# SyncE's order of loads around the second score stack, and both token parts written in slots 14 and 15

## The chip, the cores and the metric

The kernel runs on one core of one Trainium2 chip. The metric is the device time of one execution in microseconds. Three runs of the kernel before give a median of 1288.39 us (1287.05 to 1291.39).

## The reference, cut to what matters

For each of 32 batches, x is 256 tokens by 512 channels and adj is 256 by 256:

```python
h = relu(layernorm(x, eps=1e-5))
q, k, v = (split_heads(h @ W.T) for W in (Wq, Wk, Wv))      # 16 heads of 32
a = (q @ k^T) * 512**-0.5 + (adj + adj)
a = where(row of a has any nonzero, a, -inf)
p = softmax(a);  p = where(isnan(p), 0, p)
out = x + (p @ v, heads joined) @ Wo.T
```

## The kernel before, in words

Every product is made to near float32 accuracy out of halves: a matrix is kept as a high part in 16 bits and a low part (what the high part lacks), and a product is three 16-bit products. The high part is made by ScalarE, the low part by VectorE. q and k are split into two float32r parts and stacked (96 rows of three head-sized blocks), so that one matmul per half of the tokens gives a head's scores.

A batch b is worked through in 16 slots, one for each head hh. In slot hh TensorE does, in this order: the transposes of head hh's probabilities (L490), the scores of head hh+3 (L476, which in slots 13 to 15 belong to batch b+1), in even slots the value products of the two heads before (L511, L512), and then pieces of the projections named in the table `JOBS` (L401): in slots 0 to 3 the last of batch b's q, k and v; in 4 to 7, 10, 11, 14 and 15 those of batch b+1; in 8, 9, 12 and 13 the output projection of batch b-1. So heads 0 to 7 need the first stack, heads 8 to 15 the second one, whose heads 8, 9, 10 and 11 are first wanted in slots 5, 6, 7 and 8.

VectorE does in slot hh: `shift` of head hh+2 (L995: scores into `minus` with the row's bound), every fourth slot `any_nonzero` (L1016), its part of the projections that ended (`take`: L914 and L916 for q and k, L922 for v), `low_probs` of head hh (L1004) and then the extras. The extras that matter here: `tokens_stats` and `moments_of` for batch b+2 in slot 7 (L834, L843), `low_tokens(b+2, 0)` in slot 14 and its other half `low_tokens(b+1, 1)` in slot 0 of the next batch (L974, writes h_parts from h and h_parts), `low_outputs(b, 0)` in slot 15 and `low_outputs(b-1, 1)` in slot 4 (L968, writes o_parts from o and o_parts).

ScalarE does the exponentials (L725), the high parts (L736 for probabilities, L705 for outputs, L746 for tokens), the copies of products out of PSUM, and in slot 13 `copy_adj(b+1)` (L754), which waits for the shift of head 15. GpSimd does `fold` (L1223 and L1229: the sums that tell whether a row has a nonzero), `divide` (L1187 to L1203) in slots 1, 5, 9 and 13, the residual additions (L1215) and `normalise` of batch b+2 (L1163 to L1179) in slot 7.

All DMAs are issued by SyncE, one after the other, in an order written out by hand; a wait in front of one holds all behind it. A stack is twelve DMAs from SBUF to SBUF (L269), three for each group j of heads; group j of the second stack serves heads 8+j and 12+j. `stack(1, b)` waits for the last q and k product to be taken in slot 2, and has `turn_outputs(b-1, 1)` in its middle: a transposing DMA (L305) that waits for `low_outputs(b-1, 1)`. The token loads, the residual's x, the stores of y and the loads of adj stand between the stacks. The synchronisation is by semaphores. SyncE's loop runs over two batches a turn, the loops of VectorE, ScalarE and GpSimd over one; TensorE's is written out in full.

Of the kernel before, what the change touches and what calls it, by code (L numbers as in the profile page):

```python
# [14 lines left out]
HEADS = 16  # L15
# [64 lines left out]
def attention_block(nc, x, adj, wq, wk, wv, wo_t, out):  # L80
    B, N, D = x.shape
    NT = N // P
# [21 lines left out]
    with ExitStack() as ctx:  # L104
# [122 lines left out]
        def settled(engine, name):  # L227


            engine.sem_inc(went_on[name], 1)  # L230
# [18 lines left out]
        def count(kind, n, b):  # L249

            return b * PER_BATCH[kind] + (n + 1)

        def head_no(b, hh):
            return b * HEADS + hh

        @block.sync
        def _(sp):
# [31 lines left out]
            def turn_tokens(b, t, odd, first):  # L289

                sp.wait_ge(h_split, (b - 1) * NT + (t + 1))
                settled(sp, "sp")
                if not first:

                    sp.wait_ge(ended["qk"], count("qk", 0, b - 1))
                    settled(sp, "sp")
                sp.dma_start_transpose(hT[odd][:, t, :, :], h_parts[:, t, :, :].rearrange("p a d -> p (a d)")
                                       ).then_inc(h_turned[t], 16)
# [10 lines left out]
            def load_tokens(b):  # L309

                sp.wait_ge(h_ready, b)
                settled(sp, "sp")
                sp.dma_start(x_in[:, :, :], x_d[b]).then_inc(x_loaded, 16)

            def load_adj(b):

                sp.wait_ge(adj_copied, b)
                settled(sp, "sp")
                sp.dma_start(adj_in[:, :, :], adj_d[b]).then_inc(adj_loaded, 16)
# [18 lines left out]

            def body(b, odd, first, last):
                ends = last or isinstance(b, int) and b + 2 == B  # L340
                if not (first or ends):
                    load_tokens(b + 2)
                if not (first or last):
                    turn_tokens(b + 1, 1, 1 - odd, False)
                if not (first or last):
                    load_adj(b + 1)
                stack(1, b, first)
                if first:
                    load_adj(1)
                if not last:  # L350
                    stack(0, b + 1, False)
                if not ends:
                    turn_tokens(b + 2, 0, odd, False)
                if not first:
                    store(b - 1, 0)
                    store(b - 1, 1)

                    sp.dma_start(x_res[:, :, :], x_d[b]).then_inc(res_loaded, 16)
                if not last:
                    turn_outputs(b, 0)  # L360

            def store(b, t):

                sp.wait_ge(y_ready, b * NT + (t + 1))
                settled(sp, "sp")
                sp.dma_start(out_d[b, :, t, :], y[:, t, :]).then_inc(stored[t], 16)  # L366

            body(0, 0, True, False)
            with sp.Fori(1, B - 3, 2) as b:
                body(b, 1, False, False)  # L370
                body(b + 1, 0, False, False)
            body(B - 3, 1, False, False)
            body(B - 2, 0, False, False)
            body(B - 1, 1, False, True)
            for t in range(NT):

                sp.wait_ge(last_y, t + 1)
# [251 lines left out]
        def _(act):  # L629
# [32 lines left out]
            def high_out_weight(k):  # L662

                act.wait_ge(wo_leveled, k + 1)
                nc.scalar.activation(wo_hi[:, k, :], wo_in[k // 2][:, k % 2, :], ACT.Copy).then_inc(wo_high, 1)
# [82 lines left out]
            def copy_adj(b):  # L748

                act.wait_ge(adj_loaded, (b + 1) * 16)  # L750
                if not (isinstance(b, int) and b == 0):

                    act.wait_ge(shifted, head_no(b, 0))
                nc.scalar.activation(adj_now[:, :, :], adj_in[:, :, :], ACT.Copy).then_inc(adj_copied, 1)  # L754
# [22 lines left out]
            def body(b, first, nearly, last):  # L777
                for hh in range(HEADS):
                    if hh % 2:

                        if hh > 1:
                            copy_outputs(b, hh // 2 - 1, first and hh < 10)
                        elif not first:
                            copy_outputs(b - 1, PAIRS - 1, False)
                    if hh == 4:

                        take("v", 3, b, first)
                    if hh == 14 and not first:

                        take("y", 1, b - 1)  # L790
                    if hh + 1 < HEADS:
                        exponentials(b, hh + 1, first and hh + 1 < 2)
                    elif not last:
                        exponentials(b + 1, 0, False)
                    for kind, n, d in ended_before(hh, first, last):
                        if (kind, n) in (("v", 3), ("y", 1)):
                            continue
                        take(kind, n, b + d, first and (kind, d) in (("v", 0), ("qk", 0)))
                    if first and 10 <= hh < 10 + KT:

                        high_out_weight(hh - 10)
                    if hh == HEADS - 3 and not (first or last):
                        copy_adj(b + 1)
                    high_probs(b, hh, first and hh < 4)
                    if hh == HEADS - 3 and first:
                        copy_adj(b + 1)
                    if first and hh == 0:
                        split_tokens(1, True)
                    if not first and hh == 3:
                        high_outputs(b - 1, 1)  # L810
                    if not (nearly or last) and hh == 11:
                        split_tokens(b + 2, False)
                    if not last and hh == 14:
                        high_outputs(b, 0)
# [14 lines left out]
        def _(dve):  # L829
            def tokens_stats(b, tiles):  # L830

                dve.wait_ge(x_loaded, (b + 1) * 16)
                for t in tiles:
                    end = nc.vector.bn_stats(stats[:, t, :], x_in[:, t, :])  # L834
                end.then_inc(stats_done, 1)

            def moments_of(b, steps):


                dve.wait_ge(stats_done, steps)  # L840
                settled(dve, "dve")
                for t in range(NT):
                    end = nc.vector.bn_aggr(mean_var[:, t, :], stats[:, t, :])  # L843
                end.then_inc(moments, 1)
# [126 lines left out]
            def low_tokens(b, t):  # L971

                dve.wait_ge(h_high, b)
                nc.vector.scalar_tensor_tensor(h_parts[:, t, 1, :], h[:, t, :], 0.0, h_parts[:, t, 0, :],  # L974
                                               ALU.max, ALU.subtract).then_inc(h_split, 1)
# [86 lines left out]
            def body(b, first, nearly, last):  # L1062
                for hh in range(HEADS):
                    if hh + 2 < HEADS:
                        shift(b, hh + 2, first and hh + 2 < 4, first and hh + 2 < 8)
                    elif not last:
                        shift(b + 1, hh + 2 - HEADS, False)

                    if hh % 4 == 1 and not (first and hh == 1):
                        any_nonzero(*((b, hh // 4 - 1) if hh > 1 else (b - 1, QUADS - 1)), first and hh < 12)  # L1070
                    for kind, n, d in ended_before(hh, first, last):
                        take(kind, n, b + d)
                    low_probs(b, hh, first and hh < 2)
                    if not (nearly or last):
                        if hh == 7:
                            tokens_stats(b + 2, range(NT))
                            moments_of(b + 2, b + 3)
                        if hh == 14:
                            low_tokens(b + 2, 0)
                    if not first and hh == 4:  # L1080
                        low_outputs(b - 1, 1)
                    if not last and hh == 15:
                        low_outputs(b, 0)
                    if first and hh == 4:
                        out_weight_extent(1)
                        out_weight_top()
                    if first and hh == 6:
                        out_weight_scale()
                    if not (first or last) and hh == 0:
                        low_tokens(b + 1, 1)  # L1090
                    if first and hh in (1, 2):
                        low_tokens(1, hh - 1)

# [230 lines left out]
```

## Time and profile before

| what | value |
|---|---|
| median of three runs | 1288.39 us |
| the profiled execution's own time | 1287.51 us |
| its span | 1285.7 us |
| granted TensorE clock, mean | 0.993 |
| PE busy | 1191.1 us (93%) |
| DVE busy | 1082.4 us (84%) |
| ACT busy | 1026.1 us (80%) |
| POOL busy | 917.0 us (71%) |
| packets of the DMA queue that SyncE feeds | 65.2% of 16 engines' span |

Times in the rows are microseconds from the start of the span; PE is TensorE's matmul and PEld its weight load, DVE is VectorE, ACT ScalarE, POOL GpSimd, SP SyncE. 1.8 us of the profiled execution lie outside the span, and its time is 0.9 us below the median. A batch takes about 38.8 us, so 0.1 us a batch is about 3 us in all. Slot 0 of batch 15 begins at 621.18 in the trace, slot 0 of batch 16 at 659.14.

### The profile page before, as it was taken

The page shows a single profiled execution, that of the slowest core. Times are in us where ns is not written, and L with a number is a line of the kernel's source. Part 1 is how long each engine was busy: PE and PEld are TensorE (multiplying, and loading weights), DVE is VectorE, ACT ScalarE, POOL GpSimd, SP SyncE. Part 2 cuts the span into 40 slices and gives each one's busy share as a digit, 9 for nine tenths or more (in the row PEclk, how much of TensorE's full clock was granted, in tenths as well). Part 3 has the DMA queues.
Part 4 walks back from the last instruction along what each step waited for, and adds up shares of the span by engine and source line. Part 5 has one row for each costly group of instructions (what it writes and reads, how often), then busy time and mean ns, then how long its engine had stood idle before and what let it go on. Part 6 is the DMA issues. An engine that isn't in the chain of part 4 may idle for free. (4 is left out here: it accounts for less than half of the span.)

```text
span 1285.7 us, 41724 instructions
## 1 busy us (share of the span) xinstructions
PE 1191.1 (93%) x12609; PEld 998.5 (78%) x12609; DVE 1082.4 (84%) x3509; ACT 1026.1 (80%) x2399; POOL 917.0 (71%) x1272
## 2 busy tenths in 40 slices
PE   6889999999999999999999999999999999999997
PEld 5778777787778778778878777878777877777884
DVE  7888888888888888888888888888888888888885
ACT  5778887888788788877888878888877887878884
POOL 5586776777777677767777767777776777776765
PEclk9899999999999999999999999999999999999998
DMA  6566567676577675577766577765686765677742
GB/s 217 121 148 159 131 144 184 152 177 149 120 159 170 159 175 140 139 163 156 173 166 142 134 175 152 177 153 141 134 189 147 182 154 137 137 180 153 165 121 83
DMA packets 222901, 197.95 MB, mean 154 GB/s; under 512 B 146113, under 2 KB 155841, under 8 KB 222785
## 3 DMA queue, kind: packets, MB, share of 16 engines
q1 hardware_dynamic: 222784, 196.16, 65.2%
q8 instruction: 103, 1.69, 0.6%
q14 instruction: 14, 0.11, 0.0%
HBM read 46.14 MB, written 16.78 MB: 49 GB/s over the span
## 5 line engine op out<-in xcount | busy, mean ns | idle before, releaser
L725 ACT ACTIVATE probs<-minus,bounds 128x256 f32<-128x256 f32 x1024 | 464.1, 506 | 79.4 <-DVE bounds L995 78.7
L1223 POOL TENSOR_TENSOR fold<-minus 128x512 f32<-128x512 f32 x256 | 325.9, 1273 | 233.2 <-DVE bounds L995 233.0
L1004 DVE TENSOR_TENSOR pT_lo<-pT_ps,pT_hi 128x512 f16<-128x512 f32 x512 | 346.8, 677 | 120.5 <-ACT pT_hi L736 117.8
L995 DVE CUSTOM_DVE_ANT_0 minus<-s_ps,adj_now 128x256 f32<-128x256 f32 x1024 | 388.3, 415 | 9.1 <-issue 6.4
L736 ACT ACTIVATE pT_hi<-pT_ps 128x512 f16<-128x512 f32 x512 | 304.4, 595 | 65.4 <-PE pT_ps L490 62.8
L401 PE MATMUL job_ps<-hT,w_hi 128*128 128x256 f16 x2048 | 351.4, 273 | 2.9 <-DMA hT<-h_parts 2.5
L490 PE MATMUL pT_ps<-ident,probs 128*128 128x128 f32 x2048 | 309.1, 274 | 4.0 <-ACT probs L725 3.8
L476 PE MATMUL s_ps<-qk_stack 96*128 96x256 f32 x1024 | 249.5, 325 | 47.1 <-DMA qk_stack<-qk_parts 46.7
L401 PE MATMUL job_ps<-hT,w_lo 128*128 128x256 f16 x1024 | 279.4, 273 | 0.0
L490 PEld LDWEIGHTS pT_ps<-ident,probs 128*128 128x128 f32 x2048 | 244.7, 142 | 33.4 <-ACT probs L725 5.1
L1229 POOL TENSOR_TENSOR bounds<-fold 128x256 f32<-128x256 f32 x256 | 195.0, 762 | 25.1 <-POOL fold L1223 9.6
L476 PEld LDWEIGHTS s_ps<-qk_stack 96*128 96x128 f32 x1024 | 155.3, 192 | 63.0 <-DMA qk_stack<-qk_parts 62.6
L401 PEld LDWEIGHTS job_ps<-hT,w_hi 128*128 128x128 f16 x2048 | 181.0, 98 | 28.0 <-DVE v_parts L922 3.0
L401 PE MATMUL job_ps<-w_hi,hT 128*128 128x256 f16 x1016 | 193.6, 274 | 0.2 <-DVE qk_parts L916 0.2
L511 PE MATMUL o_ps<-v_parts,pT_hi 128*128 128x65 f16 x2048 | 164.1, 193 | 24.7 <-DVE pT_lo L1004 24.3
L401 PE MATMUL job_ps<-wo_hi,oT 128*128 128x512 f16 x512 | 174.6, 382 | 0.4 <-DVE oT L1102 0.3
L511 PEld LDWEIGHTS o_ps<-v_parts,pT_hi 128*128 128x128 f16 x2048 | 125.7, 97 | 44.4 <-DVE pT_lo L1004 32.2
L512 PE MATMUL o_ps<-v_parts,pT_lo 128*128 128x33 f16 x2048 | 156.4, 179 | 0.0
L401 PE MATMUL job_ps<-w_lo,hT 128*128 128x256 f16 x508 | 138.9, 274 | 0.0
L512 PEld LDWEIGHTS o_ps<-v_parts,pT_lo 128*128 128x128 f16 x2048 | 129.3, 96 | 0.1
L401 PEld LDWEIGHTS job_ps<-w_hi,hT 128*128 128x128 f16 x1016 | 97.0, 98 | 19.1 <-DVE qk_parts L916 6.3
L401 PEld LDWEIGHTS job_ps<-hT,w_lo 128*128 128x128 f16 x1024 | 100.1, 98 | 12.0
(102 smaller groups left out, 1615.5 us busy)
## 6 DMA issues: line engine op xcount, KB each, us to landing
qk_stack<-qk_parts SPq DMA_DIRECT2D x756, 128.0 KB, 2.4
x_in<-x SPq DMA_DIRECT2D x32, 512.0 KB, 4.5
x_res<-x SPq DMA_DIRECT2D x32, 512.0 KB, 4.1
out<-y SPq DMA_DIRECT2D x64, 256.0 KB, 2.3
adj_in<-adj SPq DMA_DIRECT2D x32, 256.0 KB, 4.1
qk_stack<-qk_parts SPq DMA_DIRECT2D x24, 64.0 KB, 2.0
w_in<-wq SPq DMA_DIRECT2D x2, 512.0 KB, 6.4
w_in<-wk SPq DMA_DIRECT2D x2, 512.0 KB, 8.0
```

The costliest lines, as they stand in the source:

```text
L401: end = nc.tensor.matmul(dst, lhs[a](k), rhs[c](k), start=i == 0, stop=i == len(terms) - 1)
L476: end = nc.tensor.matmul(s_ps[SCORE_BANK[hh]][:, t * N:(t + 1) * N], stack[:, 0, t * P:(t + 1) * P], stack[:, 1, :], start=True, stop=True)
L490: end = nc.tensor.transpose(pT_ps[hh % 2][:, m * N + t * P:m * N + (t + 1) * P], probs[hh % 2][:, t, m * P:(m + 1) * P], ident[:, :])
L511: nc.tensor.matmul(ps[:, 0:LOW + HD], hi, v[:, 0:LOW + HD], start=m == 0, stop=False)
L512: end = nc.tensor.matmul(ps[:, 0:HD + 1], lo, v[:, 0:HD + 1], start=False, stop=m == NT - 1)
L725: end = nc.scalar.activation(probs[hh % 2][:, t, :], minus[hh // 2 % 2][:, hh % 2, t, :], ACT.Exp, bias=bounds[:, hh // 2 % 4, 2 * (hh % 2 ...
L736: nc.scalar.activation(pT_hi[hh % 4][:, :, :], pT_ps[hh % 2][:, :].rearrange("p (m n) -> p m n", m=NT), ACT.Copy).then_inc(pT_high, 1)
L995: end = nc.vector.tensor_tensor_reduce(out=minus[pair % 2][:, hh % 2, t, :], in0=s_ps[SCORE_BANK[hh]][:, t * N:(t + 1) * N], in1=adj_now[: ...
L1004: nc.vector.tensor_tensor(pT_lo[hh % 4][:, :, :], pT_ps[hh % 2][:, :].rearrange("p (m n) -> p m n", m=NT), pT_hi[hh % 4][:, :, :], ALU.sub ...
L1223: nc.gpsimd.tensor_tensor(f1[:, :, :], src[:, :, 0:N // 2], src[:, :, N // 2:N], ALU.add).then_inc(folded1, 1)
L1229: nc.gpsimd.tensor_tensor(f2, f1[:, :, 0:N // 4], f1[:, :, N // 4:N // 2], ALU.add).then_inc(folded2, 1)
```

## The change

On SyncE, the three steps that stood ahead of the second stack go elsewhere. The token load and the load of adj run one batch further ahead (b+3 in place of b+2, b+2 in place of b+1) and come after the first stack; both transposing DMAs of batch b+2's tokens are issued together, between the two stores of y. On VectorE the second half of the token parts moves from slot 0 of the next batch to slot 15, where it comes before `low_outputs(b, 0)`; the first half stays in slot 14. One of the two tiles of the statistics moves from slot 7 to slot 3. On ScalarE `copy_adj` comes after `high_probs` in slot 13 in place of before it. Nothing of the arithmetic changes.

```diff
@@ SyncE
             def body(b, odd, first, last):
                 ends = last or isinstance(b, int) and b + 2 == B
-                if not (first or ends):
-                    load_tokens(b + 2)
-                if not (first or last):
-                    turn_tokens(b + 1, 1, 1 - odd, False)
-                if not (first or last):
-                    load_adj(b + 1)
                 stack(1, b, first)
                 if first:
                     load_adj(1)
                 if not last:
                     stack(0, b + 1, False)
-                if not ends:
-                    turn_tokens(b + 2, 0, odd, False)
+                if not (ends or isinstance(b, int) and b + 3 == B):
+                    load_tokens(b + 3)
                 if not first:
                     store(b - 1, 0)
+                if not ends:
+                    load_adj(b + 2)
+                    for t in range(NT):
+                        turn_tokens(b + 2, t, odd, False)
+                if not first:
                     store(b - 1, 1)
                     sp.dma_start(x_res[:, :, :], x_d[b]).then_inc(res_loaded, 16)
...
-            with sp.Fori(1, B - 3, 2) as b:
+            with sp.Fori(1, B - 5, 2) as b:
                 body(b, 1, False, False)
                 body(b + 1, 0, False, False)
-            body(B - 3, 1, False, False)
-            body(B - 2, 0, False, False)
-            body(B - 1, 1, False, True)
+            for b in range(B - 5, B):
+                body(b, b % 2, False, b == B - 1)
@@ ScalarE
-                    if hh == HEADS - 3 and not (first or last):
-                        copy_adj(b + 1)
                     high_probs(b, hh, first and hh < 4)
-                    if hh == HEADS - 3 and first:
+                    if hh == HEADS - 3 and not last:
                         copy_adj(b + 1)
@@ VectorE
                     low_probs(b, hh, first and hh < 2)
                     if not (nearly or last):
+                        if hh == 3:
+                            tokens_stats(b + 2, range(0, 1))
                         if hh == 7:
-                            tokens_stats(b + 2, range(NT))
-                            moments_of(b + 2, b + 3)
-                        if hh == 14:
-                            low_tokens(b + 2, 0)
+                            tokens_stats(b + 2, range(1, NT))
+                            moments_of(b + 2, 2 * (b + 2))
+                        if hh >= HEADS - NT:
+                            low_tokens(b + 2, hh - (HEADS - NT))
                     if not first and hh == 4:
                         low_outputs(b - 1, 1)
                     if not last and hh == 15:
                         low_outputs(b, 0)
...
-                    if not (first or last) and hh == 0:
-                        low_tokens(b + 1, 1)
```

## Rows read from the trace of the kernel before

**Rows 1.** Waits over the whole span: engine line, releaser, us, times, longest.

```profile
PE s_ps L476 <- DMA qk_stack<-qk_parts: 46.7, 57, 2.7
```

**Rows 2.** SyncE's timeline, batch 15: start, us in issuing, line, transfer, count.

```profile
625.74 0.41 SPq L313 DMA_DIRECT2D x_in<-x  x1
626.51 1.28 SPq L297 DMA_TRANSPOSE hT<-h_parts  x1
...
628.94 4.66 SPq L269 DMA_DIRECT2D qk_stack<-qk_parts  x6
634.06 1.27 SPq L305 DMA_TRANSPOSE oT<-o_parts  x1
635.38 3.81 SPq L269 DMA_DIRECT2D qk_stack<-qk_parts  x6
```

**Rows 3.** PE's timeline, batch 15: the scores of head 8.

```profile
634.33 0.51 PE L476 MATMUL s_ps<-qk_stack 96*128 96x256 f32 x2 [0.52 <-DMA qk_stack<-qk_parts]
```

**Rows 4.** Line L269, stack transfers: first 628.9 to 632.9, then 634.0 to 639.3.

```profile
DMA to landing us min/median/max: 3.4/3.6/4.0
...
DMA to landing us min/median/max: 2.4/2.4/2.5
```

**Rows 5.** SyncE's timeline: the transpose inside the second stack, batches 2 and 30.

```profile
126.98 1.27 SPq L305 DMA_TRANSPOSE oT<-o_parts  x1
...
1215.73 1.32 SPq L305 DMA_TRANSPOSE oT<-o_parts  x1
```

**Rows 6.** PE's timeline: head 10's scores in batches 2 and 30.

```profile
133.10 0.50 PE L476 MATMUL s_ps<-qk_stack 96*128 96x256 f32 x2 [1.48 <-DMA qk_stack<-qk_parts]
...
1220.79 0.51 PE L476 MATMUL s_ps<-qk_stack 96*128 96x256 f32 x2 [0.38 <-DMA qk_stack<-qk_parts]
```

**Rows 7.** VectorE's timeline, slot 14 of batch 15 to slot 1 of batch 16.

```profile
657.31 0.84 DVE L974 SCALAR_TENSOR_TENSOR h_parts<-h,h_parts 128x512 f16<-128x512 f32 x1
...
659.70 1.38 DVE L968 TENSOR_TENSOR o_parts<-o,o_parts 128x512 f16<-128x512 f32 x1
661.00 0.41 DVE L995 CUSTOM_DVE_ANT_0 minus<-s_ps,adj_now 128x256 f32<-128x256 f32 x1
...
662.62 0.67 DVE L974 SCALAR_TENSOR_TENSOR h_parts<-h,h_parts 128x512 f16<-128x512 f32 x1
...
664.62 0.63 DVE L1004 TENSOR_TENSOR pT_lo<-pT_ps,pT_hi 128x512 f16<-128x512 f32 x1
```

**Rows 8.** GpSimd's timeline over the same stretch.

```profile
656.98 0.62 POOL L1203 TENSOR_TENSOR o<-o_raw,factor 128x256 f32<-128x256 f32 x1
657.56 1.72 POOL L1215 TENSOR_TENSOR y<-y,x_res 128x512 f32<-128x512 f32 x1
659.25 1.27 POOL L1223 TENSOR_TENSOR fold<-minus 128x512 f32<-128x512 f32 x1
660.69 0.98 POOL L1229 TENSOR_TENSOR bounds<-fold 128x256 f32<-128x256 f32 x1 [0.17 <-POOL fold L1223]
```

**Rows 9.** PE's timeline, slot 2 of batch 16: value product of head 1.

```profile
665.32 0.20 PE L511 MATMUL o_ps<-v_parts,pT_hi 128*128 128x65 f16 x1 [0.44 <-DVE pT_lo L1004]
```

**Rows 10.** ScalarE's timeline, slot 13 of batch 15.

```profile
653.70 0.63 ACT L754 ACTIVATE adj_now<-adj_in 128x512 f32<-128x512 f32 x1 [0.67 <-DVE bounds L995]
```

**Rows 11.** VectorE's timeline, slots 7 and 9 of batch 15.

```profile
640.32 1.28 DVE L834 BATCH_NORM_STATS2 stats<-x_in 128x6 f32<-128x512 f32 x2
...
645.62 0.64 DVE L1004 TENSOR_TENSOR pT_lo<-pT_ps,pT_hi 128x512 f16<-128x512 f32 x1
```

**Rows 12.** PE's timeline, slot 10 of batch 15: last product of head 8, first of head 9.

```profile
646.07 0.19 PE L511 MATMUL o_ps<-v_parts,pT_hi 128*128 128x65 f16 x1
...
646.32 0.20 PE L511 MATMUL o_ps<-v_parts,pT_hi 128*128 128x65 f16 x1
```

**Rows 13.** Line L968 over the whole span: ns min/median/max.

```profile
L968 DVE TENSOR_TENSOR o_parts<-o,o_parts x62: 679/682/1384, 74.6 to 1251.6; 128x512 f16<-128x512 f32 x62
```

**Rows 14.** VectorE's timeline, slot 4 of batch 15.

```profile
632.67 0.69 DVE L1004 TENSOR_TENSOR pT_lo<-pT_ps,pT_hi 128x512 f16<-128x512 f32 x1 [0.59 <-ACT pT_hi L736]
```

## The prediction

> **What bounds the kernel now.** I read the shares of busy time first: TensorE is busy 93% of the span, the next engine, VectorE, 84%. So TensorE sets the time, and a change is worth what it gives or takes of TensorE's idle time. The waits say where that is: 46.7 us of it are the scores waiting for a stack transfer, 57 times [rows 1]. Over the 31 batches with a second stack fed in this way that is 1.5 us each. TensorE's timeline puts all of them in slots 5 to 8, at heads 8 to 11, those of the second stack; head 8 of batch 15 is one [rows 3]. The first stack never makes it wait.
>
> SyncE's timeline shows why head 8 is late. In batch 15 the token load, the tokens' transpose and the load of adj are issued just before the stack [rows 2]; SyncE is free in time, but their bytes are still moving, and the first stack transfers take 3.4 to 4.0 us to land where those issued later, with nothing ahead, take 2.4 [rows 4].
>
> Head 10 waits for something else. Its three transfers stand behind `turn_outputs(b-1, 1)`, which waits for VectorE's `low_outputs` in slot 4. From the issue of that transpose at 1215.73 to head 10's scores at 1220.79 are 5.06 us in batch 30 [rows 5, 6]. That is a floor, and it comes out of its parts: 1.3 us of issuing the transpose, 1.3 us for two of six transfers that take 3.81 us together [rows 2], then 2.4 us of landing [rows 4]. The same distance in batch 2 is 133.10 - 126.98 = 6.12 us. Over batches 2 to 30 (29, of which these are the first and last) it is 5.9 us in the mean and 5.0 at the least; in 17 of the 29 a delay of about 1 us in the queue falls on one of these transfers.
>
> The third place is VectorE's. From slot 14 to slot 3 it runs without a gap, and in slot 2 TensorE waits 0.44 us for the low part of head 1's probabilities [rows 9]. Whatever lengthens VectorE's work there goes into the time one to one, and head 10's floor moves with it, since slot 4 follows.
>
> **The change, part by part.**
>
> SyncE's order. With the x load, the transpose and the load of adj out of the way, the second stack's first transfers land after 2.4 to 3 us in place of 3.4 to 4, and head 8's wait (0.52 here) goes. But a gain at head 8 is real only if head 10 starts sooner, and head 10 stands at its floor: TensorE comes to it 0.5 us earlier and waits 0.5 us longer. What is left to win is the distance between 5.9 and the floor. The transfers between two second stacks are the same in number and size, so I expect the queue's delays at the same transfers: the 12 quiet batches fall to 5.05, and the 17 others, 6.25 in the mean now, keep their delay and lose some 0.15 of contention. The 12 stand at 5.4 in the mean, so they give 0.35: (12 x 0.35 + 17 x 0.15) / 29 = 0.23 us a batch. The ends are 0 and 0.85 (all at the floor).
>
> The moved transposes, loads and stores cost TensorE nothing: x and adj now land half a batch before they are read, the second transpose is issued some 1.5 us after slot 0 begins in place of 5.3 and is read in slot 4. The cover is SyncE's idle time; if it were gone, the queue would be late at the first transfer of the second stack, which has about 0.7 us to spare.
>
> The statistics. Two tiles take 1.28 us in slot 7 [rows 11]. One, 0.64, moves to slot 3. There VectorE idles 0.59 us before head 4's low part [rows 14], so it lies beside that wait and costs 0.05 at most, counted as 0. In slot 7 its absence moves VectorE's chain 0.64 us ahead until slot 9. There TensorE waits for it now without a recorded gap: head 9's first value product starts 0.25 us after head 8's last [rows 12], 0.06 after the low part that ends at 645.62 + 0.64 [rows 11]; without a wait such products stand 0.05 apart. That 0.2 us a batch goes: it lies behind head 10's stall and is a gain. Ends: 0 and 0.25.
>
> `copy_adj` behind `high_probs`. The copy waits 0.67 us for VectorE [rows 10] with `high_probs` queued behind it; now this runs in the wait. Head 13's parts come 0.5 us sooner, head 14's about 0.2 (ScalarE must then take a product that TensorE ends only in slot 14). But this gain is swallowed at once, see the next step. Counted 0; ends 0 and 0.2.
>
> The token part in slot 15. This is the step that decides. VectorE's L974 and L968 read two operands from SBUF, and the trace shows what they do beside GpSimd. `low_outputs` takes 0.68 us as a median and up to 1.384 [rows 13]. In slot 15 it takes 1.38: it starts at 659.70 under `fold` (659.25 for 1.27, so until 660.52) and ends at 661.08, 0.56 after `fold` [rows 7, 8]. That is no slower running but standing still until GpSimd is done. The other way round, L1229, 0.73 us elsewhere, takes 0.98 here: it starts at 660.69 and ends at 661.67, 0.73 after 660.94, when VectorE's reading was over. And in slot 14, `low_tokens` starts at 657.31 under GpSimd's `o` (until 657.60) and ends 0.55 after it; GpSimd's next instruction, `y`, is on record from 657.56 for 1.72 us in place of 1.27, so it was made to wait for the VectorE instruction that was there before it. All of this is the same to 0.01 us in all 29 batches. So one waits for the other's whole instruction, and the one that waits goes ahead of the other engine's next.
>
> Now two such VectorE instructions stand in a row in slot 15. The first, `low_tokens(b+2, 1)`, starts at 659.70 (this or up to 0.2 sooner, all one: `low_tokens(b+2, 0)` before it ends where GpSimd's `o` lets it, which is what swallows the 0.2 above) and ends at 661.08, as `low_outputs` does now. L1229 has waited since 660.69 and goes next, 660.94 to 661.67. `low_outputs` stands until then and ends 0.55 later, at 662.22; the shift that starts at 661.00 now starts at 662.14. That is 1.14 later. In return `low_tokens` is gone from the end of slot 0, 0.60 us of VectorE's time (the next instruction after it starts 0.60 behind it) [rows 7]. Net 0.54 us a batch, and the low part that starts at 664.62 [rows 7], for which TensorE waits [rows 9], starts 0.54 later. The ends: 0 if the pair runs back to back (1.38 + 0.60 now and then), and 0.80 if L1229 must run its 0.98 in full. I take 0.54, since it follows from both precedents.
>
> The Trainium skill (SBUF — State Buffer, Who interferes with whom) says the same as the rows: VectorE with two SBUF inputs and a GpSimd instruction that reads SBUF exclude each other for a whole instruction, and issue order decides who blocks. It speaks against this change: L1229, issued first, would hold off `low_outputs`. By the rule the trace agrees, down to the 0.25 us by which L1229 is longer; without it I would have put the move at 0.
>
> The sum: 29 x (0.54 - 0.23 - 0.20) = 29 x 0.11 = +3.2 us. The first batch is paid once: its slot 3 may wait for the third token load; I put 0.6 us, an estimate of about one tile's statistics. Against the profiled execution: 1287.5 + 3.8 = 1291.3. The median is 0.9 above that execution, so 1288.4 + 3.8 = 1292.2; I say 1292. What a measurement of this kernel can tell from no change is about 0.3%, 3.9 us, so the forecast stands on that edge.
>
> **The rivals.**
>
> VectorE keeps the port. If its next instruction is granted before GpSimd's waiting one, the pair costs nothing, and the change is faster: 29 x (0 - 0.23 - 0.20) + 0.6 = -12 us, 1276. For it: VectorE's instructions follow each other with an overlap of 0.08 us. Against: in slot 14 GpSimd's instructions do as well, and VectorE's waiting one went ahead. It decides as soon as `low_outputs` in slot 15 takes under 1 us. Chance 0.17.
>
> The first token part slips ahead. It starts at 657.31 now, GpSimd's `o` at 656.98. If the moved copy brings it 0.33 forward, not 0.2, it runs first, and everything to slot 1 is about 0.7 sooner than in my sum, fold included: 29 x (0.54 - 0.66 - 0.43) + 0.6 = -15 us, 1273. For it, ScalarE's wait of 0.67 [rows 10] is long enough; against it, the product that must be taken between. Chance 0.10.
>
> Head 10 isn't a floor, and the 46.7 us of waits go: 29 x (0.54 - 0.20 - 1.5) + 0.6 = -33 us, 1255. Batch 30 at 5.06 speaks against it. Chance 0.05.
>
> Both gains fail: the queue's delays fall more often on head 10's transfers, or slot 10 waits still. Then 29 x 0.54 + 0.6 = +16 us, 1304. Chance 0.10.
>
> **How the numbers follow.** My own case has 0.58, with its own range of 1286 to 1298 (0.1 to 0.15 us a batch either way is 3 to 4 us, the queue's delays as much again). About half of it is slower by over 0.3%, 0.03 of it faster, the rest neither. Slower: 0.29 + 0.10 = 0.39; faster: 0.17 + 0.10 + 0.05 + 0.02 = 0.34; within 0.3%: 0.27. The range is 1272 to 1298: it holds my case, the first rival and most of the second, and leaves out 1255 and 1304.
>
> **What would show it.** In the changed kernel's trace: in slot 15 L974 takes 1.38 us and L968 then about 1.2 (0.68 would be the first rival); L974 in slot 14 takes about 1.05 in place of 0.84 (0.68 would be the second). Head 8's scores no longer wait, head 10's wait 0.6 us or more in nearly every batch, 5.05 us behind the transpose's issue in the quiet ones. The wait in slot 2 grows by 0.5 us. Slot 10 is 0.2 us shorter. The prediction is wrong above all if the two VectorE instructions don't meet GpSimd's as now, or if the low outputs of slot 4 aren't later by the same 0.54.

## The result and the profile after

| | kernel before | changed kernel |
|---|---|---|
| median of nine runs each | 1288.69 us (1284.94 to 1293.88) | 1298.39 us (1294.92 to 1304.21) |
| profiled span | 1285.7 us | 1296.6 us |
| granted TensorE clock, mean | 0.993 | 0.986 |

The ratio is 1.0076, with a 95% interval from 1.0051 to 1.0101: slower by 0.8%. The forecast was 1292 us with a range of 1272 to 1298: the direction was right, the slowing was 10 us where 4 were forecast, and the time lies just above the range. In the ratio of the experiment with the token part alone, one execution of ten (1367.73 us at a granted clock of 0.848, a slower state that only it fell into) is left out.

The page's first part, busy time, share and instructions of each engine:

```profile
PE 1197.7 (92%) x12609; PEld 1001.5 (77%) x12609; DVE 1101.9 (85%) x3509; ACT 1029.7 (79%) x2399; POOL 917.1 (71%) x1272
```

PE and DVE are both busier with the same instructions: each kind of work has grown longer somewhere. VectorE's timeline from slot 14 of batch 15, which answers to [rows 7] (slot 0 of batch 16 begins at 663.7 here):

```profile
662.06 1.07 DVE L970 SCALAR_TENSOR_TENSOR h_parts<-h,h_parts 128x512 f16<-128x512 f32 x1
...
664.68 1.38 DVE L970 SCALAR_TENSOR_TENSOR h_parts<-h,h_parts 128x512 f16<-128x512 f32 x1
665.98 1.22 DVE L964 TENSOR_TENSOR o_parts<-o,o_parts 128x512 f16<-128x512 f32 x1
667.12 0.41 DVE L991 CUSTOM_DVE_ANT_0 minus<-s_ps,adj_now 128x256 f32<-128x256 f32 x1
...
670.14 0.64 DVE L1000 TENSOR_TENSOR pT_lo<-pT_ps,pT_hi 128x512 f16<-128x512 f32 x1
```

And GpSimd's, which answers to [rows 8]:

```profile
661.97 0.62 POOL L1199 TENSOR_TENSOR o<-o_raw,factor 128x256 f32<-128x256 f32 x1
662.55 1.72 POOL L1211 TENSOR_TENSOR y<-y,x_res 128x512 f32<-128x512 f32 x1
664.24 1.27 POOL L1219 TENSOR_TENSOR fold<-minus 128x512 f32<-128x512 f32 x1
665.67 0.98 POOL L1225 TENSOR_TENSOR bounds<-fold 128x256 f32<-128x256 f32 x1 [0.17 <-POOL fold L1219]
```

The reader sees the pair as it was forecast: the token part 1.38 us under `fold`, then GpSimd's L1225, then the output part, 1.22 us. TensorE's wait in slot 2, which answers to [rows 9]:

```profile
670.83 0.20 PE L509 MATMUL o_ps<-v_parts,pT_hi 128*128 128x65 f16 x1 [0.77 <-DVE pT_lo L1000]
```

It is 0.77 us in place of 0.44; the slots before it are longer too. The waits over the span, which answer to [rows 1]:

```profile
PE s_ps L474 <- DMA qk_stack<-qk_parts: 46.4, 38, 2.5
PE o_ps L509 <- DVE pT_lo L1000: 24.6, 32, 0.8
```

The scores wait as long in all as before, but 38 times in place of 57. Head 8 hardly waits any more; head 10 waits in every batch from 2 to 30. SyncE's timeline of batch 15 (slot 0 at 625.4) answers to [rows 2], and the landing of its first stack transfers to [rows 4]:

```profile
634.09 4.64 SPq L269 DMA_DIRECT2D qk_stack<-qk_parts  x6
639.19 1.28 SPq L305 DMA_TRANSPOSE oT<-o_parts  x1
```

```profile
L269 SPq DMA_DIRECT2D qk_stack<-qk_parts x6: 585/604/1386, 634.1 to 638.1; - x6
...
DMA to landing us min/median/max: 2.3/2.6/3.2
```

With nothing ahead they land after 2.6 us in place of 3.6. In this batch head 10 waits 0.90 us. In batch 18 it waits much longer. TensorE's timeline around slot 7 there; the figure in brackets is the idle time before the row:

```profile
758.38 0.38 PE L399 MATMUL job_ps<-hT,w_hi 128*128 128x256 f16 x2
758.60 0.27 PE L399 MATMUL job_ps<-hT,w_lo 128*128 128x256 f16 x1
758.71 0.60 PE L488 MATMUL pT_ps<-ident,probs 128*128 128x128 f32 x4
761.74 0.53 PE L474 MATMUL s_ps<-qk_stack 96*128 96x256 f32 x2 [2.43 <-DMA qk_stack<-qk_parts]
762.08 0.64 PE L399 MATMUL job_ps<-hT,w_hi 128*128 128x256 f16 x2
762.51 0.42 PE L399 MATMUL job_ps<-hT,w_lo 128*128 128x256 f16 x1
...
764.65 1.01 PE L488 MATMUL pT_ps<-ident,probs 128*128 128x128 f32 x4
```

Behind the wait the same products take 0.64 and 0.42 us where they took 0.38 and 0.27 ahead of it, the transposes 1.01 where they took 0.60, and two products start 0.43 us apart (762.08, 762.51) in place of 0.22. The same stretch in windows: length, busy time of PE, PEld, DVE, ACT and POOL, granted clock, share of the DMA engines, GB/s.

```profile
758.00:763.50 5.50, 3.07 (x22) 2.35 (x20) 3.99 (x15) 2.21 (x6) 4.62 (x10) 0.87 0.61 138
763.50:768.00 4.50, 4.50 (x40) 3.49 (x39) 2.33 (x8) 2.52 (x6) 1.63 (x3) 0.78 0.03 6
768.00:782.80 14.80, 14.80 (x153) 11.97 (x153) 10.91 (x36) 13.64 (x30) 11.47 (x16) 1.00 0.69 176
```

The granted clock fell, to the lower level of 1.2 GHz for part of the first two windows, and was whole again in the third. In the third window TensorE is busy all the time, so nothing makes up for it.

That is where the time went. Over batches 2 to 30 of the changed kernel, 17 take 38.2 to 38.7 us, five 39.0 to 39.9, and seven 41.2 to 41.6; before, all 29 lie between 37.4 and 39.7. In the seven (2, 6, 7, 11, 18, 22, 23) head 10 waited 2.15 to 2.53 us and products at half clock follow. Slots 7 and 8 together take 8.60 us there in the mean. Batch 28 waited 2.49 us with no fall behind it and takes 7.18 for the two. So a fall costs about 1.4 us, and seven of them 10 us. (Slots 7 and 8 less the batch's own wait take 6.28 us in the seven and 4.72 in the mean of the others, which gives 1.6 us; whole batches less that wait, 39.06 and 37.67, give 1.4. Seven falls are 10 to 11 us.)

This is not one execution's accident: the mean granted clock is 0.979 to 0.988 in all nine executions of the changed kernel, and 0.986 to 0.995 in those of the kernel before.

By stretches of the batch (means of batches 2 to 29, us):

| slots | before | after | difference | forecast |
|---|---|---|---|---|
| 14 to 3, the port | 14.45 | 15.00 | +0.55 | +0.54 |
| 4 to 9, the second stack | 15.37 | 15.44 | +0.07 | -0.23 |
| 10 | 2.64 | 2.45 | -0.20 | -0.20 |
| 11 to 13 | 6.42 | 6.42 | 0.00 | 0 |

The row of the second stack without the seven falls (7 x 1.4 / 28 = 0.35 a batch) is -0.28. Within the first row slot 14 is 0.42 us shorter (2.86, 2.44) and slots 0 to 3 are 0.95 longer (9.59, 10.55).

### The profile page after: what moved, and what is told of

The parts are those of the page before. It is cut to its first block and busy times, and to the rows that moved or that the text cites. A ratio compares the mean times of both kernels' runs of the same rounds, so it can differ in the third digit from the quotient of the medians.

```text
span 1296.6 us, 41683 instructions
## 1 busy us (share of the span) xinstructions
PE 1197.7 (92%) x12609; PEld 1001.5 (77%) x12609; DVE 1101.9 (85%) x3509; ACT 1029.7 (79%) x2399; POOL 917.1 (71%) x1272
## 5 line engine op out<-in xcount | busy, mean ns | idle before, releaser
L399 PE MATMUL job_ps<-hT,w_hi 128*128 128x256 f16 x2048 | 355.8, 276 | 0.1
L488 PE MATMUL pT_ps<-ident,probs 128*128 128x128 f32 x2048 | 312.9, 276 | 10.1 <-ACT probs L723 9.9
L474 PE MATMUL s_ps<-qk_stack 96*128 96x256 f32 x1024 | 251.1, 327 | 47.0 <-DMA qk_stack<-qk_parts 46.4
L399 PE MATMUL job_ps<-hT,w_lo 128*128 128x256 f16 x1024 | 282.3, 276 | 0.0
L1225 POOL TENSOR_TENSOR bounds<-fold 128x256 f32<-128x256 f32 x256 | 195.1, 762 | 25.1 <-POOL fold L1219 9.6
```

Source lines behind the costliest of these rows:

```text
L399: end = nc.tensor.matmul(dst, lhs[a](k), rhs[c](k), start=i == 0, stop=i == len(terms) - 1)
L474: end = nc.tensor.matmul(s_ps[SCORE_BANK[hh]][:, t * N:(t + 1) * N], stack[:, 0, t * P:(t + 1) * P], stack[:, 1, :], start=True, stop=True)
L488: end = nc.tensor.transpose(pT_ps[hh % 2][:, m * N + t * P:m * N + (t + 1) * P], probs[hh % 2][:, t, m * P:(m + 1) * P], ident[:, :])
L1225: nc.gpsimd.tensor_tensor(f2, f1[:, :, 0:N // 4], f1[:, :, N // 4:N // 2], ALU.add).then_inc(folded2, 1)
```

## The experiments

Each ratio is to the kernel before, with its 95% interval. The kernel before was measured again beside each group of experiments, with medians of 1289.75, 1291.84 and 1292.45 us; so experiments are compared with the changed kernel (1.0076) by their ratios, and differences in us between medians are rough by some 3 us. What is said of slots and batches is of the profiled execution.

**Work added in the wait.** The changed kernel, with eight products of the weights by themselves in front of head 10's scores. Their sums land in the bank of those scores and are overwritten by them.

```diff
             def scores(b, hh, early=False):
+                if not early and hh == HH + 2:
+                    pe.wait_ge(shifted, head_no(b, hh) + (1 - bank_before(hh)))
+                    for i in range(8):
+                        nc.tensor.matmul(s_ps[SCORE_BANK[hh]][:, 0:N], w_hi[WV][:, 0, 0:P], w_hi[WV][:, 0, 0:N],
+                                         start=True, stop=True)
```

> The changed kernel, with eight 16-bit products of 128 by 256 put in front of head 10's scores in slot 7, where TensorE waits for the stack; they write the bank that the scores overwrite, so the output is the same. Eight of them take about 0.9 us, and a quiet batch waits 0.8 to 0.9 us there. Clock theory: in the changed kernel the seven batches whose stall at head 10 is over 2.1 us run the next slots at half clock and take 41.2 to 41.6 us in place of about 39.4; with the engine kept busy in part of the stall the clock stays at 1.00 there and the time falls by 7 x 2 = 14 us, to 1284, although work was added. Queue theory (the late transfers alone cost the time, and the low clock is a mere symptom): nothing is won, 1298 to 1305, by 0 to 0.2 us a batch of added work.

Measured: 1289.4 us, 0.9993 [0.9963, 1.0023], granted clock 0.995 in the mean. The rival, by which the transfers alone set the time, is out. 256 more products made the kernel 9 us faster than the changed one by the medians, and 14 by the profiled spans: 10 of the 14 lie in batches 2 to 30, 3 before them and 1 behind. The clock theory had forecast 1284 us, 14 less. Batch 9 in TensorE's timeline:

```profile
399.18 1.04 PE L467 MATMUL s_ps<-w_hi 128*128 128x256 f16 x8
401.68 0.51 PE L480 MATMUL s_ps<-qk_stack 96*128 96x256 f32 x2 [1.47 <-DMA qk_stack<-qk_parts]
402.03 0.39 PE L399 MATMUL job_ps<-hT,w_hi 128*128 128x256 f16 x2
402.26 0.27 PE L399 MATMUL job_ps<-hT,w_lo 128*128 128x256 f16 x1
```

The added work fills the first part of a wait of 2.4 us, and the products behind it run at the whole clock. No batch from 2 to 30 is over 39.9 us, and the clock falls in none of them. The late transfers have not gone: in seven batches head 10 still waits 1.29 to 1.56 us behind the added work, some 2.2 to 2.4 us with it. Over the span:

```profile
PE s_ps L480 <- DMA qk_stack<-qk_parts: 18.4, 24, 1.6
```

18.4 us and 0.87 us of added work in each of batches 2 to 30 (slots 7 and 8 take 5.30 us in a quiet batch, 4.43 where nothing waits) are 44 us, near the 46.4 of the changed kernel. What went is the clock's part.

**Only the token part.** The kernel before, with its second token part in slot 15.

```diff
-                        if hh == 14:
-                            low_tokens(b + 2, 0)
+                        if hh >= HEADS - NT:
+                            low_tokens(b + 2, hh - (HEADS - NT))
...
-                    if not (first or last) and hh == 0:
-                        low_tokens(b + 1, 1)
```

> The kernel before, with the second token part moved from slot 0 to slot 15 and nothing else. Port theory: in slot 15 L974 takes 1.38 us and L968 1.22 us; the wait for head 1's low part in slot 2 grows by 0.5 us, and the time grows by 29 x 0.54 = 16 us over the kernel before, to 1304. Rival (VectorE's lateness is absorbed before TensorE waits for it): within 3 us of 1288. Head 8 keeps its wait, so no stall gets over 2 us that was not before, and the clock stays.

Measured: 1295.28 us, 1.0049 [1.0029, 1.007]. The direction is right; the size is 0.5%, 6 us, of the 16 forecast. VectorE's timeline, slot 15:

```profile
662.99 1.38 DVE L974 SCALAR_TENSOR_TENSOR h_parts<-h,h_parts 128x512 f16<-128x512 f32 x1
664.29 1.22 DVE L968 TENSOR_TENSOR o_parts<-o,o_parts 128x512 f16<-128x512 f32 x1
```

The pair is the same with the old order of SyncE, and slots 0 to 3 grow by 0.54 us as forecast. But slots 4 and 5 give 0.30 back. TensorE reaches slot 5 0.44 us later after slot 0 begins, but head 8's transfers have landed only 0.19 later, late for a reason of their own, so that wait shrinks by 0.16 us a batch. Another 0.09 is a wait of slot 4 for the transposed tokens (2.5 us in four batches), which is all but gone. A delay ahead of a wait with another cause is partly free. I had left that out. Nor did the clock stay, as I had expected: it fell to the lower level in batches 4 and 27 (41.55 and 41.25 us), behind waits of only 1.86 and 1.76 us. Those two falls are some 3 us of the time.

**Only the statistics.** The kernel before, with one statistics tile in slot 3.

```diff
+                        if hh == 3:
+                            tokens_stats(b + 2, range(0, 1))
                         if hh == 7:
-                            tokens_stats(b + 2, range(NT))
-                            moments_of(b + 2, b + 3)
+                            tokens_stats(b + 2, range(1, NT))
+                            moments_of(b + 2, 2 * (b + 2))
```

> The kernel before, with one tile of the statistics moved from slot 7 to slot 3 and nothing else. The prediction's term: slot 10 falls from 2.64 to 2.44 us, 29 x 0.2 = 6 us less than before, 1283, ratio 0.9955. Rival (hidden anyway): slot 10 stays and the ratio is 1.000.

Measured: 1287.78 us, 0.997 [0.9946, 0.9994]. The interval holds the forecast of 0.9955 and leaves out the rival's 1.000, if barely. In the profiled execution slot 10 falls from 2.64 to 2.45 as forecast; slots 4 and 5 take 0.17 us more, and the sum over a batch stays (38.88 before, 38.87 here). The trace puts nearly all of the 0.17 on transfers: TensorE waits in slot 4 for the transposed tokens in nine batches where it did in four (+0.07 us a batch), and 0.09 longer at head 8. None of these waits ends with VectorE. So nothing shows that the tile in slot 3 costs time; single executions of one kernel differ by as much as this gain (1279.48 to 1293.61 us here), and a pair of profiles can't decide it.

**The token part back.** The changed kernel, with that part in slot 0 again (the edit of the second experiment, reversed).

> The changed kernel with the second token part back in slot 0 of the next batch; the order of the DMAs, the split statistics and the copy of adj stay. Port theory: 29 x 0.54 = 16 us less than the changed kernel, 1282. Clock theory adds: the stall at head 10 is set by the distance from the low outputs of slot 4 to the third transfer, and that does not move, so some seven batches still fall to half clock. Rival (the order of the DMAs is what costs, not the port): no more than 3 us less than 1298.

Measured: 1302.1 us, 1.0101 [1.0073, 1.0128], where I expected a gain. SyncE's timeline of batch 15 (slot 0 at 626.9) tells why:

```profile
626.59 6.29 SPq L297 DMA_TRANSPOSE hT<-h_parts  x2
633.12 0.37 SPq L365 DMA_DIRECT2D out<-y  x1
633.67 0.39 SPq L357 DMA_DIRECT2D x_res<-x  x1
634.18 1.24 SPq L305 DMA_TRANSPOSE oT<-o_parts  x1
636.17 4.55 SPq L269 DMA_DIRECT2D qk_stack<-qk_parts  x6
```

The second transpose of the tokens waits for the part that slot 0 makes now, and the store, the load of x and a third transpose queue behind it, right ahead of the stack. The waits show it:

```profile
PE s_ps L474 <- DMA qk_stack<-qk_parts: 67.0, 46, 2.7
```

Slots 14 to 3 do give their 0.54 us back (14.46, as before), but slot 5 takes 4.13 us in place of 2.06, and the clock falls in eight of the batches from 2 to 30, now behind head 8's waits. So the place of the token part, which costs 0.54 us of port, is also what keeps the queue clear ahead of the stack. The two can't be judged apart in this order.

**The outputs' transpose one group later.** Head 10's three transfers stand behind this transpose. The changed kernel, with it after the third group of the stack.

```diff
-                    if half == 1 and j == 1 and not first:
+                    if half == 1 and j == 2 and not first:
```

> The changed kernel with the transpose of the outputs inside the second stack moved one group on, behind head 10's transfers (j == 2 in place of j == 1). Floor theory: head 10's transfers are then issued at about 12.6 us after slot 0 in place of 15.2, its stall goes, slot 7 falls from 3.73 to about 2.0 us and slot 8 from 2.67 to 2.43; no stall is left that could bring the clock down; 29 x 2.0 = 57 us less, about 1241. Rival (a next floor is close behind: head 11, whose transfers now stand behind the transpose, or VectorE): 1265 or more.

Measured: 1265.43 us, 0.9806 [0.9751, 0.9861]. Head 10's wait is gone (slot 7 takes 2.07 us), and head 11 waits in its place (slot 8 takes 3.29):

```profile
PE s_ps L474 <- DMA qk_stack<-qk_parts: 25.1, 39, 2.2
```

The floor moved by one head, as the rival had it; the 1241 of the floor theory was missed. In batch 11 the clock falls once more, behind head 11's wait of 1.96 us.

**Behind the whole stack.** The same line, with `j == G - 1`.

> The changed kernel with the transpose of the outputs behind all four groups of the second stack. With it one group on, head 10's stall went and head 11's took its place (slot 8 at 3.29 us in place of 2.43), as its transfers stood behind the transpose. Floor theory: now no transfer of the stack stands behind it, slot 8 falls to about 2.45 us, 0.85 us a batch, 25 us less than one group on: 1240. Rival: the transposed outputs are read in slot 9; issued some 17 us after slot 0 they land at 21, and if that is too late TensorE waits in slot 9 instead, and the time stays above 1255.

Measured: 1237.99 us, 0.9583 [0.9542, 0.9623]:

```profile
PE s_ps L474 <- DMA qk_stack<-qk_parts: 6.8, 11, 2.6
```

One transpose moved behind six transfers takes some 60 us from the changed kernel, 4.9% by the ratios; 1240 us were forecast. It costs nothing where it stands now: its outputs are first read in slot 8, and slots 8 and 9 are at 2.47 and 1.99 us.

**The same edit on the kernel before.**

> The kernel before, with the transpose of the outputs behind all four groups of the second stack and nothing else. Floor theory: head 10's and 11's stalls go (0.67 + 0.07 us a batch in slots 7 and 8), head 8's stays at 0.95 us since the x load, a transpose and the load of adj still stand ahead of the stack: 29 x 0.7 = 20 us less than before, 1269. So the new order of the DMAs is worth the rest, 0.9 us a batch, only where the floor at head 10 is gone. Rival: with the floor gone head 8's stall is made good later and the time comes near the 1238 of the changed kernel with the same edit.

Measured: 1277.28 us, 0.9881 [0.9824, 0.9937]:

```profile
PE s_ps L476 <- DMA qk_stack<-qk_parts: 29.1, 40, 1.9
```

Heads 10 and 11 no longer wait, head 8 still does (slot 5 takes 3.08 us), and slot 10 grows from 2.64 to 2.98, since VectorE's late statistics are now exposed. A batch is only 0.09 us shorter, and most of what the profiled span lost lies in the first two batches and in the last. The forecast, 1269, left slot 10 out. The edit is worth 1.2% here and 4.9% on the changed kernel, so other parts of the change are what lets it pay. The slots say which: with the edit in both, slots 4 to 9 take 14.95 us here and 13.54 there (above all head 8's wait, which the order of the loads takes away), and slot 10 2.98 and 2.45 (the split statistics). Neither part was added alone.

**Both token parts earlier.** The changed kernel, with the parts in slots 11 and 13, where VectorE has idle time.

```diff
-                        if hh >= HEADS - NT:
-                            low_tokens(b + 2, hh - (HEADS - NT))
+                        if hh in (11, 13):
+                            low_tokens(b + 2, (hh - 11) // 2)
```

> The changed kernel with the two token parts of VectorE in slots 11 and 13 in place of 14 and 15, where VectorE waits 0.7 to 1 us a slot and GpSimd is less in the way; the order of the DMAs stays. Port theory: low_outputs in slot 15 takes 1.4 us in place of 1.38 + 1.22 for both, the chain of slots 14 to 3 is 0.5 us shorter, 29 x 0.5 = 15 us less than the changed kernel: 1283; the stalls at head 10 over 2.1 us and the low clock after them stay. Rival (VectorE's order, not the port, is what costs): the parts delay shifts of slots 12 to 14 instead, and the time stays within 4 us of 1298.

Measured: 1271.38 us, 0.9848 [0.9803, 0.9893], 27 us less than the changed kernel (2.3 points by the ratios), where I expected 15. Slots 14 to 3 take 14.15 us in place of 15.00, 0.85 less and not 0.5, and that although the low outputs of slot 15 take 1.75 us where 1.4 was forecast; so the forecast's account of this stretch was not right. Slots 0 and 1 are at 2.44 and 2.22 us, slot 2 at 3.17 in place of 3.62. The falls of the clock stay: there are eight in the 29 batches from 2 to 30, and these take 40.1 us or more.

**Both edits.** The transpose behind the stack and the parts in slots 11 and 13.

> Both at once: transpose behind the whole second stack, token parts in slots 11 and 13. If stall and port are separate terms the gains add: 1240 - 15 = 1225. If they are two names for one wait, it is no better than the first alone, 1240.

Measured: 1206.12 us, 0.9337 [0.9298, 0.9377]. The two gains are 4.9 and 2.3 points of the ratio, 7.2 together; measured are 7.4 (92 us). They add, so they are two terms and not one. My 1225 was too high because it took 15 us for the parts. What is left is slot 2, and the low outputs of slot 15, which still wait for GpSimd (1.73 us at 618.60 in this trace, where they take 0.68 undisturbed):

```profile
PE o_ps L509 <- DVE pT_lo L1000: 10.4, 30, 0.6
...
L964 DVE TENSOR_TENSOR o_parts<-o,o_parts x62: 681/682/1791, 73.1 to 1175.2; 128x512 f16<-128x512 f32 x62
```

**The low outputs one slot later.** The kernel of the last experiment, with `low_outputs(b, 0)` at the end of slot 0 of the next batch.

```diff
-                    if not last and hh == 15:
-                        low_outputs(b, 0)
+                    if not first and hh == 0:
+                        low_outputs(b - 1, 0)
```

> The version with the transpose behind the stack and the token parts in slots 11 and 13, with low_outputs moved from slot 15 to the end of slot 0 of the next batch. There it takes 1.7 us, as GpSimd's y addition and fold go before it. Port theory: at 3.5 us after slot 0 GpSimd waits for VectorE, so it takes 0.68, VectorE's chain is 1 us shorter, and slot 2, now 0.6 us too long, falls to its 2.55 us: 29 x 0.6 = 17 us less than 1206, 1189. Rival: the wait in slot 2 is VectorE's amount of work and not the port: nothing changes, 1206.

Measured: 1187.58 us, 0.9191 [0.9149, 0.9234]. VectorE and GpSimd around slot 0 of batch 16 (at 609.8), first the one, then the other:

```profile
612.42 0.79 DVE L964 TENSOR_TENSOR o_parts<-o,o_parts 128x512 f16<-128x512 f32 x1
```

```profile
610.47 1.29 POOL L1219 TENSOR_TENSOR fold<-minus 128x512 f32<-128x512 f32 x1
611.93 0.74 POOL L1225 TENSOR_TENSOR bounds<-fold 128x256 f32<-128x256 f32 x1 [0.17 <-POOL fold L1219]
613.98 1.28 POOL L1219 TENSOR_TENSOR fold<-minus 128x512 f32<-128x512 f32 x1 [1.31 <-DVE bounds L991]
```

The output part waits only for the end of L1225 and takes 0.79 us, where it took some 1.7 in slot 15 of the last experiment. Slot 2 falls from 3.14 to 2.56 us, as the port theory had it, and 1189 us were forecast. The page of this kernel:

```profile
PE 1159.3 (98%) x12609; PEld 992.8 (84%) x12609; DVE 1072.6 (90%) x3509; ACT 1025.6 (86%) x2399; POOL 920.8 (78%) x1272
```

TensorE is busy 98% of a span of 1186.2 us, and a batch takes 35.7 us in the mean. This kernel is 8% faster than the one before and the fastest of the study.

## Why the prediction was wrong

- **What bounds the kernel.** Right: TensorE's idle time behind the second stack and behind VectorE's chain. Taking both away gave 8%.
- **Head 8's wait goes.** Right. Summed over the batches it fell from 19 us to 0.5.
- **Head 10's floor.** That it is one was right, and so was its height; that the mean came out right was in part luck. From the transpose's issue to head 10's scores are 5.61 us in the mean in place of 5.88: -0.27, and -0.23 was forecast. The quiet batches stand at 4.96 to 5.27, 5.07 in the mean (5.05 was forecast). But the delayed ones were to stay 17 and to lose 0.15 us from their 6.25. They are 12, and at 6.38; with 17 of them the mean would be 5.83, a gain of 0.05. Why there are fewer is open.
- **The token part in slot 15.** Right to 0.02 us: 1.07, 1.38 and 1.22 us where 1.05, 1.38 and about 1.2 were forecast, and +0.55 us over slots 14 to 3. The rivals by which VectorE keeps the port or the first part slips ahead are out.
- **The statistics.** Slot 10 gave 0.20 us, as forecast, in this kernel and in the one with the statistics alone. The copy of adj was counted at nothing, and that holds as far as the traces go: in the kernel with the token part back, which keeps that move, slot 14 is 0.41 us shorter than before and slots 0 to 3 are 0.41 longer, so that slots 14 to 3 take 14.46 us where they took 14.45. It was not tried alone.
- **The step that failed** is in the passage on SyncE's order: "TensorE comes to it 0.5 us earlier and waits 0.5 us longer." As a sum of idle time that holds. But it takes a wait of 0.5 at head 8 and one of 1.5 at head 10 for the same as one of 2. They aren't: behind seven of the eight waits of over 2.1 us the clock fell to 1.2 GHz, and a fall cost 1.4 us, 10 us in all. The added products of the first experiment show the idle wait as the cause: head 10's transfers have landed 19.25 us after slot 0 begins, in the changed kernel 19.44, but TensorE works in the first 0.9 us, no wait for the stack is above 1.6 us, and the falls are gone. The Trainium skill (TensorE: Matmul & The Clock Gate, HAM oscillation — how this bites in real kernels) describes a kernel whose waits for transfers send TensorE back to its lower clock before each group of products. The trace agrees with the order of events, a wait and then the lower clock, but the waits on that page are longer; here 2.15 to 2.53 us were enough in seven of eight cases, and batch 28's 2.49 us were not. The trace of before held a warning as well: one wait of 2.24 us in the last batch, at 1257.4, with products at half clock behind it (its row is in the last section). I didn't weigh it, and no rival held this mechanism. The rival at 1304 is the nearest number, but its reason is out: both gains came.
- **The sum.** The profiled span grew by 10.9 us: +3.2 for the 29 batches as forecast, +10 for the clock, -1.3 up to slot 0 of batch 2 where +0.6 was forecast, and -0.7 from slot 0 of the last batch on. That is 11.2. What is measured for the 29 batches is +12.9; how it splits into the forecast's 3.2 and the clock's 10 rests on the cost of a fall, and with 1.6 us for one it would be 2 and 11.

Two of my expectations failed for the same reason as the prediction, an effect on a neighbour that I had priced at nothing: the token part back in slot 0 held up the queue, and the token part alone was partly covered by head 8's wait.

## What to carry to other kernels

When a change merges two waits of TensorE into one, ask what the clock does behind the longer one; the sum of idle time doesn't tell. For a transfer that is late, look at what stands between it and its predecessors in the queue: one transpose moved behind the stack gave 4.9% on the changed kernel and 1.2% on the old one, so an order that loses by itself can be half of one that wins. Keep VectorE's instructions with two inputs in SBUF out of the stretches in which GpSimd works, and count a move among them by both engines' timelines.

## What was not expected of the hardware

In the changed kernel's batches 2 to 30 a wait of 2.15 to 2.53 us in an otherwise whole stream of products was followed by half clock in seven of eight cases, and none of 1.91 us or less was. The kernel before has the same at 1257.40, where even the scores take 0.79 us in place of 0.5:

```profile
1257.40 0.79 PE L476 MATMUL s_ps<-qk_stack 96*128 96x256 f32 x2 [2.24 <-DMA qk_stack<-qk_parts]
```

The length alone doesn't decide, and 1.91 is no safe length. Other kernels fell behind shorter waits: 1.76 and 1.86 us with the token part alone, 1.77 with the statistics alone, 1.92 with the transpose last on the kernel before, 1.96 with it one group later. Batch 27 of the kernel with the token part alone:

```profile
1110.83 0.50 PE L476 MATMUL s_ps<-qk_stack 96*128 96x256 f32 x2 [1.76 <-DMA qk_stack<-qk_parts]
1111.17 0.39 PE L401 MATMUL job_ps<-hT,w_hi 128*128 128x256 f16 x2
1111.40 0.31 PE L401 MATMUL job_ps<-hT,w_lo 128*128 128x256 f16 x1
1111.51 0.63 PE L401 MATMUL job_ps<-hT,w_hi 128*128 128x256 f16 x2
```

And waits of 1.86 us (the kernel before, batch 23), 2.64 (token parts in slots 11 and 13) and 2.71 (token part back) passed without a fall. What else decides is open. Eight added products, about 0.9 us, were enough to keep the clock.

The queue of SyncE shows a delay of about 1 us at some transfer (issues of 1.4 and 1.6 us, at most 2.3, where the median is 0.60), on changing transfers from batch to batch; its cause is open.
